# A four-layer graph network on one core: layer 1's attention weights from two exponentiated rows and a minimum with the mask

## The reference

```python
x = _layernorm(x + _L0_gnn_ref(x, adj, ...), axis=-1)
x = _layernorm(x + _L1_gnn_ref(x, adj, ...), axis=-1)
x = _layernorm(x + _L2_gnn_ref(x, adj, ...), axis=-1)
x = _layernorm(x + _L3_gnn_ref(x, L3_gnn_adj, adj, ...), axis=-1)
```

```python
h = jnp.einsum('bnf,fo->bno', x, W)
s1 = h @ a1
s2 = h @ a2
e = jax.nn.leaky_relu(s1[:, :, None] + s2[:, None, :], negative_slope=ALPHA)   # ALPHA = 0.2
att = jnp.where(adj > 0, e, jnp.float32(NEG_BIG))
att = jax.nn.softmax(att, axis=1)
h_prime = jnp.einsum('bij,bjo->bio', att, h)
return jax.nn.elu(h_prime)
```

## Time and profile before

| what | value |
|---|---|
| median of the runs shown | 473.56 us (472.64 to 473.72) |
| the profiled execution | 474.5 us, span 472.7 us |
| PE busy | 383.9 us (81%) |
| DVE busy | 378.8 us (80%) |
| ACT busy | 358.2 us (76%) |
| POOL busy | 295.4 us (62%) |
| ACT, exponentials of edges (L649), 64 | 48.4 us |
| mean granted PE clock | 0.928 of full speed |

### The profile page before, as it was taken

How to read it: one execution, slowest core, us unless ns; L and a number is a source line. 1 busy time by engine, 2 the same in 40 slices (tenths; PEclk the granted TensorE clock), 3 DMA queues, 4 the chain that set the end, 5 groups by cost and what they waited for, 6 DMA issues and landing times. The chain is left out here.

```text
span 472.7 us, 9315 instructions
## 1 busy us (share of the span) xinstructions
PE 383.9 (81%) x2818; PEld 338.3 (72%) x2825; DVE 378.8 (80%) x1384; ACT 358.2 (76%) x869; POOL 295.4 (62%) x425
## 2 busy tenths in 40 slices
PE   4489999999777687687687889899999959889870
PEld 3379999998667587587687778789889855545440
DVE  0067888888988799999999864688889896888862
ACT  1367999999876879889889845677778757787864
POOL 4117888877455354464453575477777785778883
PEclk9789999999978988998897979899999999999995
DMA  6997563000000000000000000000000000011112
GB/s 149 239 248 183 113 136 74 2 0 1 3 1 1 1 1 1 2 0 1 1 2 0 3 1 0 2 2 1 1 2 1 2 1 1 1 67 68 67 71 91
DMA packets 8757, 18.21 MB, mean 39 GB/s; under 512 B 1280, under 2 KB 2560, under 8 KB 8704
## 3 DMA queue, kind: packets, MB, share of 16 engines
q0 software_dynamic: 2304, 8.39, 9.4%
q1 hardware_dynamic: 2976, 4.52, 3.0%
q10 hardware_dynamic: 3424, 4.66, 2.8%
HBM read 21.76 MB, written 4.19 MB: 55 GB/s over the span
## 5 line engine op out<-in xcount | busy, mean ns | idle before, releaser
L459 PE MATMUL o_ps<-h_scaled,PT 128*128 128x129 f32 (+1 forms) x1536 | 191.0, 286 | 12.5 <-DVE y L947 9.6
L459 PEld LDWEIGHTS o_ps<-h_scaled,PT 128*128 128x128 f32 x1536 | 186.4, 202 | 13.8 <-issue 10.1
L676 ACT ACTIVATE X<-y,offset,rstd 128x128 f32<-128x128 f32 x256 | 104.7, 480 | 21.4 <-POOL offset L268 21.3
L897 DVE SCALAR_TENSOR_TENSOR PT<-rows_ps,factors,MT 128x512 f32<-128x512 f32 x128 | 88.9, 736 | 0.0
L401 PE MATMUL h_ps<-wx,xT 128*128 128x130 f32 x384 | 68.5, 321 | 2.9 <-DVE smax L863 1.6
L259 POOL TENSOR_TENSOR rstd<-var_eps,neg_half 128x4 f32<-128x4 f32 x64 | 66.4, 1038 | 5.0
L401 PEld LDWEIGHTS h_ps<-wx,xT 128*128 128x128 f32 x384 | 59.0, 220 | 11.5 <-issue 10.2
L967 DVE BATCH_NORM_STATS2 stats<-y 128x6 f32<-128x128 f32 x256 | 55.9, 280 | 6.6
L649 ACT ACTIVATE edge<-edge,col_tmp,col_full 128x512 f32<-128x512 f32 x64 | 48.4, 802 | 14.4 <-DVE edge L875 14.4
L249 POOL TENSOR_TENSOR h_scaled<-hx,factors 128x516 f32<-128x516 f32 x32 | 33.6, 1051 | 28.7 <-PE o_ps L459 15.5
L249 POOL TENSOR_TENSOR h_scaled<-hx,col_tmp 128x512 f32<-128x512 f32 x16 | 16.7, 1042 | 55.8 <-DVE col_tmp L915 55.8
(11 more groups left out here) (99 smaller groups left out, 711.7 us busy)
## 6 DMA issues: line engine op xcount, KB each, us to landing
MT<-adj_by_j POOLq DMA_DIRECT2D x16, 512.0 KB, 8.5
X<-x SPq DMA_DIRECT2D x16, 256.0 KB, 6.0
out<-X ACTq DMA_DIRECT2D x16, 256.0 KB, 2.0
w_rel<-w SPq DMA_DIRECT2D x1, 256.0 KB, 3.3
w_back<-w_by_output ACTq DMA_DIRECT2D x1, 192.0 KB, 3.4
wx<-w_by_input ACTq DMA_DIRECT2D x1, 192.0 KB, 3.7
bias<-b ACTq DMA_DIRECT2D x1, 64.0 KB, 2.9
bias<-b SPq DMA_DIRECT2D x1, 64.0 KB, 7.7
```

Source lines behind the costliest of these rows:

```text
L459: last = pe.matmul(o_ps[it.b][:, ic, first:1 + D], PT[:, it.b, jc, ic * P:(ic + 1) * P], h_scaled[:, it.b, jc, first:1 + D], start=(jc == ...
L676: last = act.activation(X[:, g, c, :], y[:, b, c, :], ACT.Identity, bias=offset[:, b, c:c + 1], scale=rstd[:, b, c:c + 1])
L897: dve.scalar_tensor_tensor(out=PT[:, it.b, c, :], in0=rows_ps[:], scalar=factors[:, it.b, 1, c:c + 1], in1=m, op0=ALU.max, op1=ALU.mult, * ...
```

## The change

For layer 1, ACT no longer takes exponentials of edges. With M the maximum of s1, `node_terms` computes two columns of 4 numbers a partition: BELOW = max(s1 - M, -430) and ABOVE = max(s2 + M, 0). PE spreads BELOW in place of s1. `take_rows` takes two exponentials of that row over 512 numbers: q = exp(0.2 * row) into `q_rows`, and r = exp(row) in place in `rows_ps`. ACT's `column_hinge` gives U = exp(-0.8 * ABOVE), DVE's `column_weight` takes max(U, `big_col`), where `big_col` is 3e38 for a column without edges. An entry is then max(q U, r), which is at most 1 for a column with edges, and the weight is min(max(mask, empty), that), again with the sum over i. The order within a slot changes on DVE: the four weights of layer 1 stand together, and `add_elu`, the statistics and the aggregation of `at(-1)` move to the end of the slot, behind the column work.

```diff
             def take_rows(it):
...
-                act.activation(q_rows[:, :], rows_ps[:], ACT.Copy, scale=SLOPE).then_inc(sem("rows_taken"), 1)
+                act.activation(q_rows[:, :], rows_ps[:], ACT.Exp, scale=SLOPE)
+                act.activation(rows_ps[:], rows_ps[:], ACT.Exp).then_inc(sem("rows_taken"), 1)
-            def column_exponents(it):
-                act.wait_ge(sem("smax"), it.done)
-                act.activation(shifts[:, it.b, 0:2], shift_k[:, 3:5], ACT.Copy, scale=smax[:, it.b:it.b + 1])\
-                    .then_inc(sem("shifts"), 1)
-                act.wait_ge(sem("shifts"), it.done)
-                act.activation(col_tmp[:, it.b, EXPONENT, :], hx[:, it.r, :, S2], ACT.Relu, scale=1 - SLOPE,
-                               bias=shifts[:, it.b, 0:1]).then_inc(sem("exponent"), 1)
+            def column_hinge(it):
+                act.wait_ge(sem("above"), it.of_layer)
+                act.activation(col_tmp[:, it.b, HINGE, :], col_tmp[:, it.b, ABOVE, :], ACT.Exp, scale=SLOPE - 1)\
+                    .then_inc(sem("hinge"), 1)
-            def column_terms(it):
-                t = col_tmp[:, it.b, :, :]
-
-                dve.wait_ge(sem("exponent"), it.of_layer)
-                dve.scalar_tensor_tensor(out=t[:, BIAS, :], in0=t[:, EXPONENT, :], scalar=shifts[:, it.b, 1:2],
-                                         in1=minus_full[:, it.g, :], op0=ALU.add, op1=ALU.mult)\
-                    .then_inc(sem("col_bias"), 1)
-
+            def node_terms(it):
+
+                dve.wait_ge(sem("smax"), it.done)
+                if it.g >= 2:
+                    dve.wait_ge(sem("rows_ps"), it.done - 2)
+                dve.tensor_scalar(col_tmp[:, it.b, BELOW, :], hx[:, it.r, :, S1], smax[:, it.b:it.b + 1], LOWEST,
+                                  ALU.subtract, ALU.max).then_inc(sem("below"), 1)
+                dve.tensor_scalar(col_tmp[:, it.b, ABOVE, :], hx[:, it.r, :, S2], smax[:, it.b:it.b + 1], 0.0,
+                                  ALU.add, ALU.max).then_inc(sem("above"), 1)
+
+            def column_weight(it):
+
+                dve.wait_ge(sem("hinge"), it.of_layer)
+                dve.wait_ge(sem("big_col"), it.of_layer)
+                dve.tensor_tensor(col_tmp[:, it.b, WEIGHT, :], col_tmp[:, it.b, HINGE, :], big_col[:, it.g, :],
+                                  ALU.max).then_inc(sem("col_weight"), 1)
+
+            def edges(it):
                 dve.wait_ge(sem("rows_taken"), it.of_layer)
+                dve.wait_ge(sem("col_weight"), it.of_layer)
                 for c in range(C):
-                    dve.scalar_tensor_tensor(out=edge[:, c, :], in0=rows_ps[:], scalar=t[:, R_EIGHTY, c:c + 1],
-                                             in1=q_rows[:, :], op0=ALU.add, op1=ALU.max)\
-                        .then_inc(sem("edge_lin"), 1)
+                    dve.scalar_tensor_tensor(out=edge[:, c, :], in0=q_rows[:, :],
+                                             scalar=col_tmp[:, it.b, WEIGHT, c:c + 1], in1=rows_ps[:],
+                                             op0=ALU.mult, op1=ALU.max).then_inc(sem("edge_lin"), 1)
...
                     if it.l == 1:
-                        dve.wait_ge(sem("edge"), it.g * C + (c + 1))
+                        dve.wait_ge(sem("edge_lin"), it.g * C + (c + 1))
                         dve.scalar_tensor_tensor(out=PT[:, it.b, c, :], in0=m, scalar=empty_col[:, it.g, c:c + 1],
-                                                 in1=edge[:, c, :], op0=ALU.max, op1=ALU.mult,
+                                                 in1=edge[:, c, :], op0=ALU.max, op1=ALU.min,
```

More of the change, by code:

```diff
@@ L27 @@
 LAST_ATTENTION, ATTENTION_END = G * LAYERS - 4, G * LAYERS + 3
-R_EIGHTY, EXPONENT, BIAS, Z, RZ = range(5)
+R_EIGHTY, EXPONENT, BIAS, Z, RZ, ABOVE, BELOW, HINGE, WEIGHT = range(9)
+LOWEST, BIG = -430.0, 3e38
 class Item:
@@ L124, in build @@
         minus_full = sb("minus_full", [P, G, C])
+        big_col = sb("big_col", [P, G, C])
         flag_int = sb("flag_int", [P, 1], I32)
@@ L434, in spread_rows @@
                 if it.l == 1:
-                    pe.wait_ge(sem("hx"), it.done)
+                    pe.wait_ge(sem("below"), it.of_layer)
                 else:
@@ L444, in spread_rows @@
                 for c in range(C):
-                    col = hx[:, it.r, c, S1:S1 + 1] if it.l == 1 else factors[:, it.b, 0, c:c + 1]
+                    col = col_tmp[:, it.b, BELOW, c:c + 1] if it.l == 1 else factors[:, it.b, 0, c:c + 1]
                     last = pe.transpose(rows_ps[:, c * P:(c + 1) * P], col.broadcast_to([P, P]), ident[:])
@@ L641, in take_rows @@
                     act.wait_ge(sem("edge_lin"), (it.of_layer - 1) * C)
-                act.activation(q_rows[:, :], rows_ps[:], ACT.Copy, scale=SLOPE).then_inc(sem("rows_taken"), 1)
-            def edges(it, cs):
-                if cs[0] == 0:
-                    act.wait_ge(sem("col_bias"), it.of_layer)
-                for c in cs:
-                    act.wait_ge(sem("edge_lin"), it.g * C + (c + 1))
-                    act.activation(edge[:, c, :], edge[:, c, :], ACT.Exp, bias=col_tmp[:, it.b, BIAS, c:c + 1],
-                                   scale=col_full[:, it.g, c:c + 1]).then_inc(sem("edge"), 1)
+                act.activation(q_rows[:, :], rows_ps[:], ACT.Exp, scale=SLOPE)
+                act.activation(rows_ps[:], rows_ps[:], ACT.Exp).then_inc(sem("rows_taken"), 1)
             def elu(it):
@@ L697, in attention_slot @@
                     elu(at(-1))
-                if at(1) and at(1).l == 1:
-                    edges(at(1), (0, 1))
                 if at(2) and at(2).l in (0, 2):
@@ L702, in attention_slot @@
                 if at(2) and at(2).l == 1:
-                    column_exponents(at(2))
+                    column_hinge(at(2))
                 if at(-1) and at(-1).l == 2:
                     elu(at(-1))
-                if at(1) and at(1).l == 1:
-                    edges(at(1), (2, 3))
                 if at(-3) and at(-3).l != 1:
@@ L853, in own_max @@
                 dve.wait_ge(sem("hx"), it.done)
-                if it.l == 1:
-                    dve.tensor_scalar(col_tmp[:, it.b, R_EIGHTY, :], hx[:, it.r, :, S2], 1 - SLOPE, None,
-                                      ALU.mult).then_inc(sem("r_eighty"), 1)
                 s = S1 if it.l == 1 else S2
@@ L1001, in attention_slot @@
                 if at(1) and at(1).l == 1:
-                    column_terms(at(1))
+                    edges(at(1))
+                if at(2) and at(2).l == 1:
+                    node_terms(at(2))
                 if at(-2) and at(-2).l == 0:
@@ L1012, in attention_slot @@
                     weights(at(1), (0, 1))
+                if at(1) and at(1).l == 1:
+                    weights(at(1), (2, 3))
                 if at(-2) and at(-2).l != 1:
                     aggregate(at(-2))
-                if at(-1) and at(-1).l == 1:
-                    add_elu(at(-1))
-                if at(-1) and at(-1).l == 1:
-                    finish(at(-1))
-                if at(1):
+                if at(1) and at(1).l != 1:
                     weights(at(1), (2, 3))
@@ L1024, in attention_slot @@
                     column_sums(at(1))
-                if at(-1) and at(-1).l == 1:
-                    aggregate(at(-1))
                 if at(1) and at(1).l == 0:
                     find_empty_columns(at(1))
+                if at(2) and at(2).l == 1:
+                    column_weight(at(2))
                 if at(1) and at(1).l == 1:
                     column_factors(at(1))
+                if at(-1) and at(-1).l == 1:
+                    add_elu(at(-1))
+                    finish(at(-1))
+                    aggregate(at(-1))
                 if n == G + 1:
```

12 lines of the change are left out of this document (4 added, 8 removed).

## The result

The changed kernel takes 485.26 us (median of 4 runs, 484.04 to 486.85), the kernel before 473.64 beside it: ratio 1.025, 95% interval 1.023 to 1.027. It is slower by 11.6 us, where a gain of 2.3 us was forecast.

The account below looks back on a forecast made before the run. DVE was taken to bound layer 1, with a loop through ACT and POOL close behind. Steady slots -3.3, clock +0.8, entering +0.7, slot 29 -1.5, leaving +1.0 gave -2.3 from 474.5; median 0.9 lower: 471.3 us (469.2 to 472.1).

Parts of the forecast that it names:

- What ACT gains: Layer 1, ACT: take_rows becomes two exponentials, the second adding 0.48 us before elu_exp.
- what DVE loses: Layer 1, DVE: its work per slot falls from 8.62 to 7.97 us, with small ops at 0.07 each.
- The loop from R to R: Layer 1: from R, the start of take_rows, through ACT and POOL to the next take_rows, 8.29 us, setting the slot.
- my -3.3: Ten steady slots of layer 1, each 0.33 us shorter than 8.62: -3.3 us.
- The step that failed: PE's projection, attention and row spread: 6.14 us at partly low clock, rows 0.2 late, four slots of ten, +0.8.
- The entering term: Slots 15 to 18: longer way from own maximum to take_max, plus the second exponential while rows come late; +0.7 us.
- rival (2): Layer 1: saving spent on low clock in every slot and at the ends, 473.7 us; stuck node term, 475.2; chance 0.34.
- Leaving: Slot 29: PE's rows come sooner, -1.5 us; slots 31 and 32: the tail stands before take_max, +1.0; together -0.5.
- (3): Layer 1: POOL's neg_mean waits behind a weight, loop 8.68 us in each slot; 473.2 to 475.6 us; chance 0.18.
- the signs of being wrong: Node terms over 0.3 us, neg_mean 0.6, q_rows waiting beyond every second slot, edges not 0.73, or take_norm held by the hinge.

Follow-up runs that it names:

- order_back: The changed kernel's arithmetic with DVE's old order: add_elu and statistics between the two pairs of weights, aggregation behind the column sums; 471.40 us, ratio 0.996.
- after_pool: The changed kernel with one POOL edit: in layer 1, find_rstd and find_offset of at(-2) stand ahead of elu_low(at(-1)); 471.66 us, ratio 0.994.
- nodes_late: order_back with node_terms moved behind take_out of layer 0; 469.37 us, ratio 0.991.
- order_mid: The changed kernel, four weights still together, with add_elu and statistics back ahead of the own maximum and aggregation behind the column sums; 477.12 us, ratio 1.007.
- pool_first: order_back with POOL's var_eps, rstd, neg_mean and offset of slot n-2 ahead of its addition to elu_exp in layer 1; 479.51 us, ratio 1.014.
- pool_above: pool_first with the second node term moved behind the first two weights on DVE, and ACT's column_hinge behind take_norm; 477.65 us, ratio 1.010.

## Why the prediction was wrong

**Right.** What ACT gains and most of what DVE loses: the second exponential follows the first after 0.47 to 0.49 us (0.48 in the sum), and the edges take 0.74 each in the steady slots. A node term takes 0.13 to 0.15 from its start to the next, twice the 0.07 of the sum. The loop from R to R is 8.33 in the slot from 195.86 on (8.29 in the forecast), ACT waits for `offset`, PE ahead of its projection, and DVE for `hx` in nine slots of ten, though 0.22 to 1.57 us and not 0.3. In order_back, where no row is late, the ten slots are at -3.0 against my -3.3. That its 471.4 us are the forecast's 471.3 is luck: it is another order, and its entering costs 2.7 where I had 0.7.

**The step that failed** is the one on PE: "it is 201.03 to 207.17 = 6.14 us: rows at R + 8.45 to 8.5, 0.2 late", four times, +0.8 (0 to 2.0). The number of late rows was nearly right, five slots of ten; the size was not. The 6.14 came from a slot in which only the first 2.4 us of that chain ran at the low level. In the changed kernel the chain begins with the low stretch, which mostly lasts 7.0 us instead of 3.6; of the chain in slot 23, 6.1 us are at the low level, and it takes 8.03 us. So the rows end at R + 10.5 and are some 2 us late, and even behind the one short stretch the chain takes 6.58 (189.24 to 195.82) and ACT waits 1.08. The term measured +10 instead of +0.8 (7.0 less the -3.0 of order_back). ACT's five waits for the rows are 7.2 of that, so each late row cost its full lateness, as the forecast priced it. For the rest it had no term: four of the five slots behind a late row take 8.74 to 8.87 from R to R and not 8.33. In these four `neg_mean` and `offset` both stand behind a weight (0.61 to 0.75 and 0.53 instead of 0.20 each; in the slot of 8.33 only `offset` does), and where the row is 1.9 late the next edges wait 0.72. That the lateness costs by the way over `elu_exp`, POOL and `offset` is what after_pool shows, which cuts that way alone: nearly the same waits for the rows, and 8.3 us less in the steady slots. Why the low stretches are longer stays open. The kernel before held a warning: in slot 29 its low stretch lasts 7.0 us too (251.0 to 258.0), and the prediction used that slot only for leaving.

**The entering term**, +0.7 (0 to 1.1), was mis-sized: +5.0. I took node terms at 0.07 each and weighed a stuck one in rival (2) for the steady slots only, where it didn't come. It came in slot 14, beside `mean_term`, where PE's attention waits for the `take_out` behind it. order_back has +2.65 there, of which nodes_late takes 2.1 away, 1.1 in slot 14 itself; the other 2.4 come with the order, 1.2 of them in slot 15 with its long low stretch.

**Leaving**: slot 29 gained 0.5 and not 1.5, and slot 30, behind a low stretch of 7.0 us, takes 10.94 against 8.63. In sum it is +0.9, where -0.5 was forecast.

**Rivals.** (2) had late rows at the low clock as the cause, in every slot, and a size of 0.2 each. (3) had the mechanism of POOL behind the weights, which did come: 0.3 to 0.9 a slot in the changed kernel, 0.4 in order_back, 0.7 in order_mid. Neither reached 485, since both kept the low stretch at its size of before. Of the signs of being wrong, two came: a node term of over 0.3 us, in slot 14, and rows that ACT waits for, in every second slot.

## What to carry to other kernels

Before work is moved behind an instruction that another engine waits for, price that engine's whole chain with the longest low-clock stretch that any part of the trace holds, laid over it from its start, and not from a slot that has a part of one. Then follow the lateness once around: if it comes back to its start without slack on the way, it costs in every slot. Cutting the way back (here four tiny instructions moved ahead of an addition on GpSimd) may be worth more than shortening the way. Read a gain by stretches before it is called a repair: about half of that one came where the kernel before was held up too. And look at what lies under what: here a long GpSimd addition was free only beside VectorE instructions that read one input from PSUM.

## What the runs showed of the hardware

- A `tensor_scalar` of 4 elements a partition, one input in SBUF, stood 1.08 to 1.28 us behind a GpSimd addition or product of two SBUF inputs, and a weight with two SBUF inputs, started 0.02 us after the addition, took 1.80 instead of 0.74. The edge instruction, one input in PSUM, wasn't held. The Trainium skill, "SBUF — State Buffer", Who interferes with whom, names `tensor_scalar` among the operations that can take the shared ports in their fast modes, and lets the first to issue hold them for its whole instruction. The rows of pool_first and pool_above agree (addition at 218.01, node term at 218.02; addition at 213.95, weight at 213.97). In slot 14 the two start 0.01 us apart, the node term first, too close to tell the order of issue.
- GpSimd's `rstd` (4 elements, 1.03 us) held nothing: in order_back it runs from 211.26, and the weight at 211.40 took its usual 0.74. So the length of an instruction on the other engine alone isn't what blocks: `rstd` is nearly as long as the addition over 512 elements (1.27), beside which the node term ended only 0.02 us after it.
- Small GpSimd instructions behind a weight wait in their turn: `neg_mean` 0.61 to 0.75 and `offset` 0.53 to 0.72 instead of 0.20.
